# Masked attention and a routed feed-forward layer: full-height selector and last partial outputs, and a triangle product on TensorE for the 256-query scores

## The reference

```python
xn = layernorm(x)                                   # 4 x 1024 x 256
q, k, v = heads(xn @ Wq.T + bq), heads(xn @ Wk.T + bk), heads(xn @ Wv.T + bv)   # 16 heads of 16
q, k = rope(q), rope(k)
att = softmax(where(tril, q @ k.T / 4, -inf))
attn = merge(att @ v) @ Wo.T + bo
idx = top_k(softmax(xn @ router_w.T + router_b), 4)     # 4 of 16 blocks of 64 hidden units
h = relu(where(block chosen, xn @ w1.T + b1, 0))        # 1024 hidden units
out = x + attn + where(block chosen, h, 0) @ w2.T + b2
```

## Time and profile before

| | |
|---|---|
| median of 3 runs | 824.03 us (823.89 to 825.13) |
| the profiled execution's own time | 824.19 us |
| its span, first to last instruction | 822.3 us |
| granted TensorE clock | 1.00 of full speed, in every slice |
| PE busy | 799.8 us, 4923 matmul records |
| DVE busy | 615.2 us |
| ACT busy | 410.3 us |
| POOL busy | 336.9 us |
| DMA | 88.11 MB, 36.4% of the 16 engines' time |

### The profile page before, as it was taken

How to read it: one execution, slowest core, us unless ns; L and a number is a source line. 1 busy time by engine, 2 the same in 40 slices (tenths; PEclk the granted TensorE clock), 3 DMA queues, 4 the chain that set the end, 5 groups by cost and what they waited for, 6 DMA issues and landing times.

```text
span 822.3 us, 14185 instructions
## 1 busy us (share of the span) xinstructions
PE 799.8 (97%) x4923; PEld 461.1 (56%) x4923; DVE 615.2 (75%) x1880; ACT 410.3 (50%) x858; POOL 336.9 (41%) x348
## 2 busy tenths in 40 slices
PE   7999999999899999999999999999999999999998
PEld 3666454444455555555655655555666556465664
DVE  6858978878999777686897967768587878768423
ACT  3513544655364565445463554545365463546462
POOL 4485058515740165639324127636802013022120
PEclk9999999999999999999999999999999999999999
DMA  8952516332334544242150636133060443310021
GB/s 261 267 167 78 155 33 180 114 92 92 86 135 110 137 138 150 80 116 91 44 170 17 163 105 180 67 110 105 35 195 26 107 116 105 84 41 15 2 71 52
DMA packets 66147, 88.11 MB, mean 107 GB/s; under 512 B 7324, under 2 KB 34972, under 8 KB 66076
## 3 DMA queue, kind: packets, MB, share of 16 engines
q1 hardware_dynamic: 66076, 87.21, 36.4%
HBM read 49.22 MB, written 37.98 MB: 106 GB/s over the span
## 4 chain that ended last, share of the span: by engine, by line
PE 81%; POOL 5%; DVE 5%; ACT 5%; issue 3%; DMA 1%; SPq 0%; ACTq 0%; DVEq 0%; POOLq 0%
PE o_bank L1250 15%; PE banks L1158 12%; PE banks L1170 12%; PE banks L1142 12%; PE banks L1232 12%; PE banks L1116 7%; ACT probs L1043 4%; PE banks L1125 3%; PE banks L1197 3%; DVE banks L1448 2%; PE banks L1236 1%; POOL pieces L896 1%; POOL hT L904 1%; PE banks L1147 1%; DVE banks L1457 1%
## 5 line engine op out<-in xcount | busy, mean ns | idle before, releaser
L1043 ACT ACTIVATE probs<-banks 128x512 f32<-128x512 f32 (+1 forms) x608 | 311.9, 580 | 280.6 <-PE banks L1236 112.8
L1232 PE MATMUL banks<-q_st,k_st 99*128 99x512 bf16 (+3 forms) x768 | 208.5, 327 | 5.8 <-ACT probs L1043 3.7
L1170 PE MATMUL banks<-k_st,q_st 96*128 96x512 bf16 (+3 forms) x768 | 211.8, 327 | 2.0 <-DVE row_max L1448 1.5
L1445 DVE TENSOR_REDUCE part_max<-banks 128x1 f32<-128x512 f32 x256 | 160.2, 678 | 12.0 <-PE banks L1170 11.5
L1448 DVE CUSTOM_DVE_ANT_0 banks<-banks,tri,part_max 128x512 f32<-128x512 f32 (+3 forms) x256 | 128.7, 555 | 54.0 <-PE banks L1170 53.6
L1142 PE MATMUL banks<-xnT,w_sb 128*128 128x256 f32 x512 | 135.7, 388 | 1.6 <-ACT probs L1043 0.7
L1448 DVE CUSTOM_DVE_ANT_0 banks<-banks,tri 128x512 f32<-128x512 f32 (+3 forms) x256 | 119.2, 512 | 20.4 <-PE banks L1170 20.0
L1250 PE MATMUL o_bank<-probs,v_sb 128*17 128x512 f32 (+3 forms) x1536 | 133.4, 487 | 0.0
L904 POOL TENSOR_TENSOR hT<-hT,gates 128x512 f32<-128x512 f32 x48 | 55.5, 1158 | 180.5 <-ACT hT L1029 152.2
L1158 PE MATMUL banks<-w_sb,hT 128*128 128x256 f32 x512 | 122.5, 383 | 2.6 <-POOL hT L904 1.8
L1232 PEld LDWEIGHTS banks<-q_st,k_st 99*128 99x128 bf16 x768 | 69.1, 97 | 77.7 <-ACT probs L1043 27.3
(11 more groups left out here) (100 smaller groups left out, 746.8 us busy)
## 6 DMA issues: line engine op xcount, KB each, us to landing
term_scratch<-pieces SPq DMA_DIRECT2D x84, 256.0 KB, 2.9
q_st<-term_scratch SPq DMA_DIRECT2D x16, 768.0 KB, 6.0
k_st<-term_scratch SPq DMA_DIRECT2D x16, 768.0 KB, 8.6
y_scratch<-o_norm SPq DMA_DIRECT2D x31, 256.0 KB, 2.5
gates<-gate_scratch SPq DMA_DIRECT2D x24, 256.0 KB, 6.3
acc<-in_x SPq DMA_DIRECT2D x8, 512.0 KB, 4.0
rope_sb<-y_scratch SPq DMA_DIRECT2D x15, 256.0 KB
out<-acc SPq DMA_DIRECT2D x7, 512.0 KB, 2.9
```

The costliest lines, as they stand in the source:

```text
L1043: nc.scalar.activation(probs[:, h:h + shared(k), PROBS_AT[u]:PROBS_AT[u] + w], bank, ACT.Exp, scale=SCALE).then_inc(s_out, 1)
L1170: nc.tensor.matmul(bank[:, 0:w], q_st[0:KROWS, at, h, i * P:(i + 1) * P], k_st[0:KROWS, at, h, c * HALF:c * HALF + w], start=True, stop=Tr ...
L1232: last = nc.tensor.matmul(bank[:, i], k_st[0:SROWS, at, h + i, j * P:(j + 1) * P], q_st[0:SROWS, at, h + i, q0:q0 + w], start=(i == 0), st ...
L1445: ins = nc.vector.tensor_reduce(part_max[:, h, at:at + 1], bank[:, 0:w], AX.X, ALU.max)
```

## The change

There are five parts.

1. `masked_late` holds for the 128-wide units alone. The 64 banks with two heads of 256 queries each get one triangle product on PE, with 2 x 128 columns, and DVE's 64 masks of that shape go. The 32 masks over four heads of 128 queries stay on DVE.
2. `sel` has 128 rows, 112 of them zero, and `chosenT` has 128 partitions, set to zero by POOL at the start; the product at L1147 (L1148 after) now runs over 128 rows. The transfer of `sel` grows from 32 to 256 KB.
3. The second product of `last_out_rest` runs over 128 rows: its weights `wo_half` have 64 zero rows and lie beside `wo_last`, and the upper 64 rows of `yT` are filled with a copy of the lower ones by one more `load_y`.
4. PE's wait for `wo_last_in` moves ahead of the rest products; the counts of `ones_set` grow by one.
5. The last four token tiles are stored one by one, not in pairs.

```diff
 def masked_late(n, k):
 
-    return diagonal(*UNITS[k]) and (width(k) <= QTR)
+    return diagonal(*UNITS[k]) and (width(k) <= P)
...
-        wo_last = x_sb[:, 0, :]
-        sel = gates[0:NBLK, 1, 0:FB // 2, :].rearrange("p a (c m) -> p (a c) m", m=P)
+        wo_last, wo_half = x_sb[:, 0, :], x_sb[:, 1, :]
+        sel = gates[:, 1, 0:FB // 2, :].rearrange("p a (c m) -> p (a c) m", m=P)
...
-        chosenT = sb("chosenT", [NBLK, T], BF16)
+        chosenT = sb("chosenT", [P, T], BF16)
...
-            def load_y(b, c, first, stop):
+            def load_y(b, c, first, stop, at=None):
...
-                at = first % 2 * GH * HD
+                at = first % 2 * GH * HD if at is None else at
...
-                    sp.dma_start(wo_last, wo_last_c).then_inc(wo_last_in, 16)
+                    sp.dma_start(x_sb[:, 0:2, :], wo_last_c).then_inc(wo_last_in, 16)
...
                     load_y(b, 1, 2, 3)
+                    load_y(b, 1, 2, 3, P // 2)
             store_out(B - 1, 0)
-            for u in range(2, 4):
-                sp.wait_ge(m_out, M_COUNT["outl", 2 * u + 1])
-                t = slice(2 * u, 2 * u + 2)
+            for t in range(NT // 2, NT):
+                sp.wait_ge(m_out, M_COUNT["outl", t])
                 sp.dma_start(out_rows[B - 1, :, t, :], acc[:, t, :]).then_inc(stored[1], 16)
...
+            nc.gpsimd.memset(chosenT[:], 0.0).then_inc(ones_set, 1)
             nc.gpsimd.memset(v_sb[:, :, :, :, HD:VW], 1.0).then_inc(ones_set, 1)
...
                 if t == NT // 2:
-                    pe.wait_ge(y_in[1], B * Y_INC)
+                    pe.wait_ge(y_in[1], B * Y_INC + 16)
+                    pe.wait_ge(wo_last_in, 16)
...
-                nc.tensor.matmul(bank[:, 0:D], yT[0:P // 2, 1, tokens], wo_sb[0:P // 2, 1, :], start=False, stop=False)
+                nc.tensor.matmul(bank[:, 0:D], yT[:, 1, tokens], wo_half, start=False, stop=False)
...
-                nc.vector.tensor_copy(chosenT[:], bank.bitcast(BF16)[0:NBLK, :]).then_inc(m_out, 1)
+                nc.vector.tensor_copy(chosenT[0:NBLK, :], bank.bitcast(BF16)[0:NBLK, :]).then_inc(m_out, 1)
...
-    sel = np.zeros((NBLK, FB, P), np.float32)
+    sel = np.zeros((P, FB, P), np.float32)
```

More of the change, by code:

```diff
@@ L743, in store_chosen @@
                 sp.wait_ge(m_out, M_COUNT["chosenT", b])
-                sp.dma_start(gate_scratch[b % 2], chosenT[:]).then_inc(chosen_out, 16)
+                sp.dma_start(gate_scratch[b % 2], chosenT[0:NBLK, :]).then_inc(chosen_out, 16)
             def load_gates(b, q):
@@ L852, in _ @@
                     load_y(b, 1, 2, 3)
+                    load_y(b, 1, 2, 3, P // 2)
             store_out(B - 1, 0)
-            for u in range(2, 4):
-                sp.wait_ge(m_out, M_COUNT["outl", 2 * u + 1])
-                t = slice(2 * u, 2 * u + 2)
+            for t in range(NT // 2, NT):
+                sp.wait_ge(m_out, M_COUNT["outl", t])
                 sp.dma_start(out_rows[B - 1, :, t, :], acc[:, t, :]).then_inc(stored[1], 16)
             sp.wait_ge(stored[0], B * 16)
-            sp.wait_ge(stored[1], (B + 1) * 16)
+            sp.wait_ge(stored[1], (B + 3) * 16)
         @block.gpsimd
@@ L947, in _ @@
             pool.wait_ge(xn_ready, NT)
-            pool.wait_ge(ones_set, 1)
+            pool.wait_ge(ones_set, 2)
             nc.gpsimd.memset(k_st[KROWS:P, :, :, :], 1.0).then_inc(ones_set, 1)
-            pool.wait_ge(ones_set, 2)
+            pool.wait_ge(ones_set, 3)
             pool.wait_ge(bias_in, 16 * 5)
@@ L955, in _ @@
             nc.gpsimd.tensor_tensor(bo_sb[:], bo_sb[:], b2_sb, ALU.add).then_inc(ones_set, 1)
-            pool.wait_ge(ones_set, 3)
+            pool.wait_ge(ones_set, 4)
             add_biases(0, 0)
@@ L1061, in _ @@
                 if what == ("v", 0, 0):
-                    act.wait_ge(ones_set, 1)
+                    act.wait_ge(ones_set, 2)
                 if what == ("hid", 0, 0, 0):
@@ L1207, in last_out_rest @@
                 nc.tensor.matmul(bank[:, 0:D], yT[:, 0, tokens], wo_sb[:, 0, :], start=True, stop=False)
-                nc.tensor.matmul(bank[:, 0:D], yT[0:P // 2, 1, tokens], wo_sb[0:P // 2, 1, :], start=False, stop=False)
+                nc.tensor.matmul(bank[:, 0:D], yT[:, 1, tokens], wo_half, start=False, stop=False)
             def last_out(t):
                 i = t - NT // 2
-                if i == 0:
-                    pe.wait_ge(wo_last_in, 16)
                 if i % 2 == 0:
@@ L1289, in _ @@
                 work(what)
-            pe.wait_ge(ones_set, 2)
+            pe.wait_ge(ones_set, 3)
             for what in STEPS:
@@ L1429, in take_chosen @@
                 bank = filled("chosenT", b)
-                if b == 1:
+                if b == 0:
+                    dve.wait_ge(ones_set, 1)
+                elif b == 1:
                     dve.wait_ge(s_out, S_COUNT["hid", 0, 3, FB - 1])
-                elif b:
+                else:
                     dve.wait_ge(chosen_out, (b - 1) * 16)
-                nc.vector.tensor_copy(chosenT[:], bank.bitcast(BF16)[0:NBLK, :]).then_inc(m_out, 1)
+                nc.vector.tensor_copy(chosenT[0:NBLK, :], bank.bitcast(BF16)[0:NBLK, :]).then_inc(m_out, 1)
             def max_unit(n, k, h):
@@ L1481, in normalise @@
                 if n == 0 and c == 0:
-                    dve.wait_ge(ones_set, 3)
+                    dve.wait_ge(ones_set, 4)
                 link(nc.vector.transpose(o_bank[:], o_bank[:]))
@@ L1631 @@
     wo_last[:, :HD] = arrays["woT"][(H - GH) * HD:].reshape(GH, HD, D)
-    arrays["wo_last"] = wo_last.reshape(P, D)
+    wo_half = np.zeros((P, D), np.float32)
+    wo_half[:P // 2] = arrays["woT"][P:P + P // 2]
+    arrays["wo_last"] = np.stack([wo_last.reshape(P, D), wo_half], axis=1)
     arrays = {f"in_{k}": np.ascontiguousarray(v) for k, v in arrays.items()}
```

## The result

The changed kernel takes 813.91 us (median of 4 runs, 813.75 to 814.15) against 824.0 us before (823.89 to 825.13). Where that touches a number it is said.

What follows compares the result with a forecast made beforehand. PE was taken to bound the kernel, with 81% of the chain of waits. Terms -7.1 - 1.5 - 0.3 - 0.3 + 7.0 - 3.0 = -5.2 us gave 819.0, stated as 818.8 us; range 814.5 to 824.5.

Steps and rivals of the forecast that it cites:

- the price of the triangle products: 64 added PE products of 256 columns at 0.11 us each, after scores: +7.0 us, bounds 6.9 to 13.4.
- what DVE gives back, -3.0: 64 masks leaving DVE free score banks sooner: -3.0 us, somewhat under half of at most 7.1; bounds -8 to +3.
- Selector, -7.1: 32 selector products after hidden blocks, at full height, no longer lay weight loads open: -7.1 us, bounds 0 and 7.4.
- The rival that height is not the cause (4%): Loads stay open at selector and last partial outputs, so neither saving comes: 827.6 us, chance 4%.
- Last partial outputs, -1.5: The 16 records before L1217 at the end take 3.5 us instead of 5.02: -1.5 us, bounds 0 to 1.6.
- stores, -0.3: Last token tiles stored singly, so the final, half-sized store ends sooner: -0.3 us, bounds 0 and 1.1.
- The tail's exponential, -0.3: In the tail, `pv` loads wait 0.72 us on an exponential; about 0.3 us of that is saved.
- The rival "DVE gives back over 8 us" (5%): Freed DVE time returns over 8 us of PE's waits: 814 us or below, chance 5%.
- that new waits come with the new order (14%): Shuffled maxima and masks make PE wait 1 to 4 us more: 823 to 825.6 us, chance 14%.
- The rival on banks held by maxima (9%): Planner lets maxima in sooner, so scores wait for banks on exponentials: 826.8 to 831.6 us, chance 9%.
- the selector at 0.11 and blocks at 0.97: Sign in the opening part's chain: selector piece 0.11 us, each block with its selector 0.97 us.
- first maxima at 44.1: Sign in the opening part: the first product for maxima moves from 46.19 to near 44.1 us.

Runs made afterwards that it cites:

- selector_only: Kernel before with one edit, selector and chosenT over 128 rows; order, masks, last outputs and stores as before: 817.0 us.
- selector64: Changed kernel with the selector over 64 rows instead of 128: 821.34 us.
- heights_only: Changed kernel with DVE masking the 256-wide scores again, planner reckoning so too; selector, last partial outputs and stores stay changed: 815.23 us.
- triangle_only: Kernel before with only the 256-wide masks moved from DVE to triangle products on PE, planner's order changing with it: 822.98 us.
- masks_new_order: Changed kernel with DVE masking the 256-wide scores again, but in the order planned as if PE did it: 824.47 us.
- all_on_pe: Changed kernel with the 128-wide masks on PE too, as 32 products of 512 columns, in a newly planned order: 832.75 us.
- handover_only: Changed kernel in the order of before, ScalarE still waiting for DVE, which adds only the triangle's last, zero column to each 256-wide bank: 815.51 us.
- detour_and_load: Changed kernel in the order of before, DVE also adding zeros at the old mask's full size to each 256-wide bank, ScalarE waiting: 818.01 us.
- load_only: Changed kernel in the order of before, DVE doing a useless reduction where the 64 masks stood, nobody waiting for it: 817.65 us.

## Why the prediction was wrong

The direction and four of six terms were right. The step that failed is the price of the triangle products: the forecast took a column added to PE to cost its full time, +7.0 us with 6.9 as the least, and the runs showed 2.8 to 4.8. The term for what DVE gives back, -3.0, was too small as well. Step by step:

- **Selector, -7.1:** right, 7.1 in `selector_only`. The rival that height is not the cause (4%) falls, and `selector64` sharpens the step: 64 rows are no better than 16. The prediction counted 96 rows as four strips of rows; of four strips in 128 rows they fill three, so its rows show that 96 goes with 128, not that equal strips are needed. The Trainium skill, "TensorE: Matmul & The Clock Gate", Part 3, says that loads overlap running products only when row groups differ. The traces do not agree: products that all use 128 rows pass at 0.86 and 0.11 us with their loads hidden, and it is 16 or 64 rows among them that cost 0.20 to 0.30 us. No run here tries row groups that have no strip in common.
- **Last partial outputs, -1.5, and stores, -0.3:** right, 1.4 and 0.4, the second no larger than the spread of the runs.
- **The tail's exponential, -0.3:** by the timeline the last `pv` run takes 2.28 us (801.26 to 803.54), was 2.54 (809.62 to 812.16), so it is right too. `heights_only`, with the masks of before, still has 2.54, and `triangle_only` 2.27.
- **Triangle products, +7.0:** mis-sized, and out of the bounds of 6.9 to 13.4. Their length is as forecast, 0.11 us. But they were charged as if PE never waited there ("a column added to PE costs its time"). Beside the masks, which is the state that the forecast started from, 64 of them cost 2.8 us; without the masks 4.8.
- **What DVE gives back, -3.0:** mis-sized, within its bounds. Taking the masks away is worth 5.9 us without triangles and 3.9 with them, the tail's 0.3 included, where 3.3 was forecast. Taken in either sequence the two parts come to -1.1 (+2.8 - 3.9, or -5.9 + 4.8), not to +3.7. The ceiling of 7.1 was not passed; taking somewhat under half of it was a guess, with no row behind it. It was also reckoned from one row alone, the 27.3 us of weight loads for scores that wait on exponentials, and that row fell by only 2.8. The loads of `pv` and the products for the maxima wait as well, 67.6 us in all, and all of these together fell by 9.5.
- **The rival "DVE gives back over 8 us" (5%):** the time came out as it said, 813.9 for "814 or below", but not in its way. The 8.1 us are reached only if the columns are charged in full: they are 3.9 that DVE gave back and 4.2 of columns that cost nothing, or, counted in the other sequence, 5.9 and 2.2. The bound of -8 on one term happened to cover the errors of two, so the result fell just below the range's end, which had been put 0.7 us inside that bound.
- **The rivals on order:** that new waits come with the new order (14%) did not happen, 0.2 us. That such a thing can decide was right in kind: `masks_new_order` lost 7 us in an order not made for it, and `all_on_pe` 15 in a new one, some 4 us of clock among them. The rival on banks held by maxima (9%) did not show: PE's waits on exponentials shrank.
- **Signs named ahead:** the selector at 0.11 and blocks at 0.97 came; first maxima at 44.1 came at 43.83, of which 0.18 is an earlier start of the blocks; rest products in 3.5 us came (3.56); DVE at 587 did not, it is 596.4, for the reason given above.

## What to carry to other kernels

Where one engine is full and yet waits for others at places, its work and those waits are not two terms of a sum: price added work at that place with the waits as they are, and take for what a faster partner gives back all who wait, not one row. Keep consecutive products at about full height, 96 to 128 rows here; rows of zeros are cheaper than a product over an eighth or a half of the array between tall ones. When a planner sets the order from costs, an edit of which it knows nothing, or an order that it has never been run in, can cost more than the edit: run the edit in the old order and the old edit in the new order.

## What the runs showed of the hardware

- A bfloat16 product of 256 columns over 16 or 64 rows, between products over 96 to 128 rows, takes 0.20 to 0.30 us more than one over 128 rows (the chains of before and `selector64` against the changed kernel's). Products over 96, 99 and 128 rows follow one another without loss. Eight float32 products that alternated 128 and 64 rows took 5.02 us, and 3.56 when all had 128.
- A DVE step over 2 elements a partition on a PSUM bank took 189 ns (`handover_only`), one over 256 took 448 (`detour_and_load`): emptying a mask of its work saved little more than half.
- The granted clock fell to its lower level, half of full speed, for some microseconds in several traces: in `masks_new_order` from 216.2 us, after a wait of PE of 2.26 us, in `load_only` from 216.2, after waits of 1.23 and 0.68 us, and in `all_on_pe` within the wait of 7.60 us. A wait of 2.05 us at the start of `masks_new_order` was not followed by such a fall, so the length of one wait does not tell it.
